# Dense build of a graph kernel: one-hot tiles stored with two pairs innermost instead of one pair's columns side by side

## The chip, the cores and the metric

The kernel runs on one core of a Trainium2 chip. The metric is the device time of one execution in microseconds. Three executions of the kernel before took 9198.9, 9200.97 and 9202.02 us, so the median is 9200.97 us.

## The reference, cut to what matters

The reference is a stack of four graph networks on 3125 nodes with 128 features (three attention layers, an edge network, two further attention layers and two convolutions), all over the same 100,000 edges:

```python
edge_index = jnp.stack([src, dst])
h = jnp.maximum(_layernorm(x, axis=-1), 0.0)
x = x + _L0_gnn_ref(h, edge_index, ...)   # per layer: softmax over the edges of a node, weighted sum of h[src]
...
# L3: per layer, msg = h[row] * dinv[row] * edge_weight * dinv[col]; agg = segment_sum(msg, col)
```

The first and the last network need, of the edges, only how many there are from each source to each destination, and the sum of their weights. The kernel therefore builds two dense matrices once, of 3200 x 3200 entries (25 x 25 cells of 128 x 128): the logarithm of the edge counts (`log_counts`) and the summed weights (`edge_weights`). Later passes read them from memory. The change touches that build alone.

## The kernel before

First the edges are sorted into cells, one cell for each block of 128 destinations and block of 128 sources. The sorted edges of a cell are cut into "pairs": a pair is a column of up to 128 edges together with the cell it belongs to. There is room for 1536 pairs. `spread_pairs` leaves, for each pair, five bf16 numbers per edge in `c.pair[:, 0..4, pair]`: the source within its block, the destination within its block, and the weight cut into three bf16 parts.

`dense_tiles` (line 678 on) then runs five engines side by side, in 96 batches of `PB = 16` pairs:

- **VectorE** writes `hot[k]`, five one-hot tiles per pair of 128 columns each, into one of two buffers, k being the batch number modulo 2. Tiles 0 and 1 compare the column numbers `iotan` with the source and the destination (L740 for the first two batches, L729 in the loop). Tiles 2 to 4 multiply tile 1 by a weight part (L744, and L733 in the loop). So there are five TENSOR_TENSOR instructions of 2048 elements per partition in a batch, 480 in all. One operand is always `value`, the numbers of `c.pair`, broadcast over the 128 columns with the column dimension innermost. Before a batch in the loop (`heat`, L724) the engine waits until TensorE has used up the batch two before, which lay in the same buffer.
- **TensorE** takes each pair of a finished batch with four bf16 matmuls of 128 x 128 x 128: three (L772) add the weights and one (L774) adds the counts. They accumulate in one of five PSUM tiles of the ring `ps`. That makes 64 matmuls per batch. Each reads one pair's tile of `hot` as the stationary operand and another as the moving one. Every fourth pair waits until ScalarE has cleared the PSUM tile.
- **ScalarE** copies each finished cell out of PSUM (L803), clears the tile of the cell before (L789), and takes the logarithm of five cells at once (L793). There are 625 cells, in 125 runs of five.
- **GpSimd** marks empty entries of each run of five cells (L714) and adds the mark to the logarithm (L717).
- **SyncE** stores each run with two DMAs of 320 KB (L819, L822).

Before the loop, GpSimd makes the constants, the first of them being `iotan` (L700, an iota of 128 numbers), and everyone waits for them. The heart of the loop before:

```python
value = c.pair[:, m, at].unsqueeze(2).to_broadcast([P, PB, P])
ve.tensor_tensor(hot[k][:, m, :, :], iotan[:, :].unsqueeze(1).to_broadcast([P, PB, P]), value, ALU.is_equal)
ins = ve.tensor_tensor(hot[k][:, m, :, :], hot[k][:, 1, :, :], value, ALU.mult)
...
pe.matmul(tile[:, 0:P], hot[k][:, 0, j, :], hot[k][:, m, j, :], start=False, stop=m == 4, skip_group_check=True)
pe.matmul(tile[:, P:2 * P], hot[k][:, 1, j, :], hot[k][:, 0, j, :], start=False, stop=True, skip_group_check=True)
```

Of the kernel before, what the change touches and what calls it, by code (L numbers as in the profile page):

```python
# [16 lines left out]
BF16 = mybir.dt.bfloat16  # L17
# [7 lines left out]
P = 128  # L25
# [27 lines left out]
PB = 16  # L53
# [623 lines left out]
def dense_tiles(nc, c, counts, weights):  # L677
# [4 lines left out]
    with ExitStack() as ctx:  # L682
        sb, pb = buffers(nc, ctx)
        iotan = sb("iotan", [P, P], BF16)
        hot = [sb(f"hot{k}", [P, 5, PB, P], BF16) for k in range(2)]
# [7 lines left out]
        with phase(nc, "consts", "hots", "hot_ready", "opened", "paired", "cleared", "copied", "marked", "begun",  # L693
# [3 lines left out]
            with nc.Block() as block:  # L697
                @block.gpsimd
                def _(g):
                    g.iota(iotan[:, :], [[1, P]], base=0, channel_multiplier=0,  # L700
# [19 lines left out]
                def _(ve):  # L720
                    ve.wait_ge(consts, 5)

                    def heat(n, k):
                        ve.wait_ge(paired, (n - 1) * PB)  # L724
                        at = bass.ds(n * PB, PB)
                        for m in range(5):
                            value = c.pair[:, m, at].unsqueeze(2).to_broadcast([P, PB, P])
                            if m < 2:
                                ve.tensor_tensor(hot[k][:, m, :, :], iotan[:, :].unsqueeze(1).to_broadcast([P, PB, P]), value, ALU.is_equal).then_inc(hots, 1)  # L729
                            else:  # L730
                                if m == 2:
                                    ve.wait_ge(hots, 2 * n + 2)
                                ins = ve.tensor_tensor(hot[k][:, m, :, :], hot[k][:, 1, :, :], value, ALU.mult)  # L733
                        ins.then_inc(hot_ready, 1)
                    for n in range(2):
                        at = slice(n * PB, (n + 1) * PB)
                        for m in range(5):
                            value = c.pair[:, m, at].unsqueeze(2).to_broadcast([P, PB, P])
                            if m < 2:
                                ve.tensor_tensor(hot[n][:, m, :, :], iotan[:, :].unsqueeze(1).to_broadcast([P, PB, P]), value, ALU.is_equal).then_inc(hots, 1)  # L740
                            else:
                                if m == 2:
                                    ve.wait_ge(hots, 2 * n + 2)
                                ins = ve.tensor_tensor(hot[n][:, m, :, :], hot[n][:, 1, :, :], value, ALU.mult)  # L744
# [6 lines left out]
                def _(pe):  # L751
# [4 lines left out]
                    with pe.Fori(0, BATCHES // 2) as i:  # L756
                        for k in range(2):
# [9 lines left out]
                            for j in range(PB):  # L767
# [3 lines left out]
                                for m in range(2, 5):  # L771
                                    pe.matmul(tile[:, 0:P], hot[k][:, 0, j, :], hot[k][:, m, j, :], start=False, stop=m == 4,  # L772
                                              skip_group_check=True)
                                pe.matmul(tile[:, P:2 * P], hot[k][:, 1, j, :], hot[k][:, 0, j, :], start=False, stop=True,  # L774
# [1257 lines left out]
```

## Time and profile before

| | |
|---|---|
| median of three runs | 9200.97 us |
| the profiled execution, own time | 9195.21 us |
| its span, first to last instruction | 9193.5 us |
| mean granted TensorE clock, whole span | 0.883 |
| busy: TensorE / VectorE / ScalarE / GpSimd | 6159.8 / 6077.5 / 3756.6 / 4016.8 us |
| dense build, first VectorE instruction to last store issued | 1402.9 to 2716.7 us |

Times in the profile are microseconds from the start of the span unless marked ns. A row of grouped instructions gives the line, the engine, the operation, `out<-in`, shapes (partitions x elements), the count, busy time and mean length in ns, and after the second bar the idle time of the engine just before them with what ended it. PEld is the weight load of TensorE, PE its matmul. The lengths of PE instructions overlap in the pipeline, so their rate is read from start to start.

### The profile page before, as it was taken

The numbers are of one execution on the slowest core, as the hardware profiler recorded it, in microseconds if no ns is written. First come the engines' busy times: TensorE is split into PE (matmuls) and PEld (weight loads), VectorE is DVE, ScalarE is ACT, GpSimd is POOL, SyncE is SP. The second block draws the span as 40 slices with busy tenths as digits, with TensorE's granted clock in tenths as the row PEclk, the third lists the DMA queues.
The fourth block names the chain that finished last, engine by engine and source line by source line (L and its number), as shares of the span: only waits on it lengthen the run. The fifth ranks groups of instructions, "written<-read, shape, count | busy, mean of one in ns | idle before, by whom it ended". The sixth has DMA issues, their size and how long they took to land. (4 is left out here: it accounts for less than half of the span.)

```text
span 9193.5 us, 178963 instructions
## 1 busy us (share of the span) xinstructions
PE 6159.8 (67%) x53418; PEld 5203.8 (57%) x53419; DVE 6077.5 (66%) x16562; ACT 3756.6 (41%) x8315; POOL 4016.8 (44%) x3723
## 2 busy tenths in 40 slices
PE   2222254444447676769999858888885888888766
PEld 2222224433437676747777637777774777777566
DVE  7444429999976565644444458888886888888722
ACT  1111101344536565634544435455543554555410
POOL 3777702456640000037777435555552555555300
PEclk9999997666668888879999979999997999999888
DMA  4111130112213232323333411111113111111345
GB/s 160 52 52 52 52 134 23 57 67 77 80 60 129 87 128 83 113 50 75 73 73 72 45 30 38 37 38 37 37 37 25 41 37 37 38 38 37 27 181 187
DMA packets 472947, 619.50 MB, mean 67 GB/s; under 512 B 283562, under 2 KB 381655, under 8 KB 453589
## 3 DMA queue, kind: packets, MB, share of 16 engines
q1 hardware_dynamic: 362948, 414.53, 13.6%
q0 software_dynamic: 109568, 200.53, 10.3%
q14 instruction: 320, 2.61, 0.1%
q8 instruction: 111, 1.82, 0.1%
HBM read 468.42 MB, written 146.37 MB: 67 GB/s over the span
## 5 line engine op out<-in xcount | busy, mean ns | idle before, releaser
L976 POOL DMA_INDIRECT rows<-source_table,idxb x2640 | 2540.4, 962 | 3043.5 <-ACT idxb L996 1314.6
L1589 DVE CUSTOM_DVE_ANT_0 junk<-pen,ps_top 128x512 f32<-128x512 f32 x1760 | 1136.3, 682 | 140.1 <-PE ps_top L1745 139.6
L772 PE MATMUL ps_cells<-hot 128*128 128x128 bf16 x4608 | 576.1, 284 | 716.3 <-DVE hot L733 629.0
L772 PEld LDWEIGHTS ps_cells<-hot 128*128 128x128 bf16 x4608 | 464.5, 133 | 755.9 <-issue 751.8
L360 POOL DMA_INDIRECT records<-recb,idxb x784 | 762.8, 973 | 256.0 <-issue 246.5
L733 DVE TENSOR_TENSOR hot<-hot,pair 128x2048 bf16<-128x2048 bf16 x282 | 778.1, 2812 | 13.4
L714 POOL TENSOR_SCALAR none<-logs 128x640 f32<-128x640 f32 x125 | 459.2, 3673 | 616.2 <-ACT logs L793 612.9
L1745 PE MATMUL ps_top<-srow,sel 128*128 128x128 bf16 x7040 | 622.6, 224 | 124.5 <-ACT srow L1649 93.1
L388 PE MATMUL ps_g<-hott 64*128 64x128 bf16 x784 | 101.1, 308 | 718.9 <-ACT hott L404 714.8
L1745 PEld LDWEIGHTS ps_top<-srow,sel 128*128 128x128 bf16 x7040 | 448.6, 104 | 233.1 <-issue 153.2
L1708 PEld LDWEIGHTS ps_e<-ident,rows 128*128 128x128 f32 x3520 | 522.5, 213 | 77.0 <-issue 18.9
L1081 PE MATMUL ps_acc<-rows,pt 128*128 128x131 f32 x3750 | 560.0, 296 | 0.0
L803 ACT ACTIVATE both<-ps_cells 128x256 f32<-128x256 f32 x625 | 236.0, 381 | 722.1 <-PE ps_cells L774 715.6
L1759 PE MATMUL ps_acc<-val,hot 128*128 128x132 f32 x3520 | 505.2, 288 | 32.9 <-DVE val L1551 32.4
L1002 PE MATMUL ps_tgt<-identb,dlob 128*128 128x128 bf16 x2640 | 340.4, 231 | 275.3 <-issue 172.1
L1708 PE MATMUL ps_e<-ident,rows 128*128 128x128 f32 x3520 | 519.3, 297 | 3.9 <-DMA rows<-source_table,idxb 3.9
L1093 PE MATMUL ps_t<-ident,y 128*128 128x128 f32 x1875 | 345.9, 311 | 261.0 <-ACT y L1122 261.0
L1081 PEld LDWEIGHTS ps_acc<-rows,pt 128*128 128x128 f32 x3750 | 518.6, 211 | 0.0
L1644 ACT ACTIVATE dist<-ps_tgt,minus_p 128x512 f32<-128x512 f32 x440 | 302.3, 687 | 509.5 <-PE ps_tgt L1002 508.6
L1548 DVE TENSOR_TENSOR val<-rows,p 128x512 f32<-128x512 f32 x440 | 304.8, 693 | 311.0 <-issue 309.3
L388 PEld LDWEIGHTS ps_g<-hott 64*128 64x128 bf16 x784 | 75.2, 138 | 742.1 <-ACT hott L404 739.1
L729 DVE TENSOR_TENSOR hot<-iotan,pair 128x2048 bf16<-128x2048 bf16 x188 | 494.6, 2669 | 0.0
(311 smaller groups left out, 15449.7 us busy)
## 6 DMA issues: line engine op xcount, KB each, us to landing
logs<-log_counts SPq DMA_DIRECT2D x75, 1600.0 KB
wt<-edge_weights SPq DMA_DIRECT2D x50, 1600.0 KB
rows<-source_table,idxb POOLq DMA_INDIRECT x2640
edge_weights<-both SPq DMA_DIRECT2D x125, 320.0 KB, 2.8
log_counts<-none SPq DMA_DIRECT2D x125, 320.0 KB, 2.2
records<-blank SPq DMA_DIRECT2D x16, 1870.0 KB
feat<-records SPq DMA_DIRECT2D x220, 128.0 KB, 2.4
rb<-records SPq DMA_DIRECT2D x6, 4352.0 KB
```

What stands on the lines that cost most here:

```text
L360: g.indirect_dma_start(out=recs[:, :], out_offset=bass.IndirectOffsetOnAxis(ap=idxb[k][:, t:t + 1], axis=0), in_=recb[k][:, t, :], in_offs ...
L714: g.tensor_scalar(none[r][:, :, :], logs[r][:, :, :], -1.0, -BIG, ALU.is_lt, ALU.mult).then_inc(marked, 1)
L729: ve.tensor_tensor(hot[k][:, m, :, :], iotan[:, :].unsqueeze(1).to_broadcast([P, PB, P]), value, ALU.is_equal).then_inc(hots, 1)
L733: ins = ve.tensor_tensor(hot[k][:, m, :, :], hot[k][:, 1, :, :], value, ALU.mult)
L772: pe.matmul(tile[:, 0:P], hot[k][:, 0, j, :], hot[k][:, m, j, :], start=False, stop=m == 4, skip_group_check=True)
L976: g.indirect_dma_start(out=rows[r][:, k, :], out_offset=None, in_=table, in_offset=bass.IndirectOffsetOnAxis(ap=idxb[r][:, k:k + 1], axis= ...
L1081: ins = pe.matmul(ps_acc[b % 2][:, 0:GA], pt[n % 4][:, t, :], c.rows[:, at, 0:GA], start=at == 0, stop=at == NB - 1)
L1093: ins = pe.transpose(ps_t[n % 4][:, t, :], y[b % 2][:, at * P:(at + 1) * P], c.ident[:, :])
L1589: ve.tensor_tensor_reduce(out=junk[h % 2][:, :], in0=pen[mk][:, :], in1=ps_top[h % 2][:, :], scale=1.0, scalar=-BIG, op0=ALU.add, op1=ALU.max,
L1708: ins = pe.matmul(ps_e[:, q * P:(q + 1) * P], rows[r][:, q, :], c.ident[:, :], start=False, stop=q == TG - 1)
L1745: ins = pe.matmul(ps_top[h % 2][:, q * P:(q + 1) * P], sel[:, q * HEADS + h, :], srow[:, :], start=True, stop=True)
L1759: ins = pe.matmul(ps_acc[:, 0:HEADS * HW], hot[r][:, q, :], val[k][:, q * HEADS:(q + 1) * HEADS, :].rearrange("p h f -> p (h f)"), start=q ...
```

## The change

The tiles of a batch are stored as 8 couples of pairs, and within a couple the two pairs' values alternate element by element: column 0 of both pairs, column 1 of both, and so on. `iotan` doubles to 128 x 2 elements, each column number twice. The broadcast `value` now has the couple's two numbers innermost, repeated over 128 columns. TensorE reads one pair out of a couple with a step of two elements (4 bytes). Counts, shapes in elements, waits and order of all instructions stay as they were.

```diff
-        iotan = sb("iotan", [P, P], BF16)
-        hot = [sb(f"hot{k}", [P, 5, PB, P], BF16) for k in range(2)]
+        iotan = sb("iotan", [P, P, 2], BF16)
+        hot = [sb(f"hot{k}", [P, 5, PB // 2, P, 2], BF16) for k in range(2)]
...
-                    g.iota(iotan[:, :], [[1, P]], base=0, channel_multiplier=0,
+                    g.iota(iotan[:, :, :], [[1, P], [0, 2]], base=0, channel_multiplier=0,
...
-                            value = c.pair[:, m, at].unsqueeze(2).to_broadcast([P, PB, P])
+                            value = c.pair[:, m, at].rearrange("p (a j) -> p a j", j=2).unsqueeze(2).to_broadcast([P, PB // 2, P, 2])
                             if m < 2:
-                                ve.tensor_tensor(hot[k][:, m, :, :], iotan[:, :].unsqueeze(1).to_broadcast([P, PB, P]), value, ALU.is_equal).then_inc(hots, 1)
+                                ve.tensor_tensor(hot[k][:, m, :, :, :], iotan[:, :, :].unsqueeze(1).to_broadcast([P, PB // 2, P, 2]), value, ALU.is_equal).then_inc(hots, 1)
                             else:
                                 if m == 2:
                                     ve.wait_ge(hots, 2 * n + 2)
-                                ins = ve.tensor_tensor(hot[k][:, m, :, :], hot[k][:, 1, :, :], value, ALU.mult)
+                                ins = ve.tensor_tensor(hot[k][:, m, :, :, :], hot[k][:, 1, :, :, :], value, ALU.mult)
...
-                                    pe.matmul(tile[:, 0:P], hot[k][:, 0, j, :], hot[k][:, m, j, :], start=False, stop=m == 4,
+                                    pe.matmul(tile[:, 0:P], hot[k][:, 0, j // 2, :, j % 2], hot[k][:, m, j // 2, :, j % 2], start=False, stop=m == 4,
                                               skip_group_check=True)
-                                pe.matmul(tile[:, P:2 * P], hot[k][:, 1, j, :], hot[k][:, 0, j, :], start=False, stop=True,
+                                pe.matmul(tile[:, P:2 * P], hot[k][:, 1, j // 2, :, j % 2], hot[k][:, 0, j // 2, :, j % 2], start=False, stop=True,
                                           skip_group_check=True).then_inc(paired, 1)
```

The first two batches (L740, L744) change in the same way.

## Rows read from the trace of the kernel before

**Rows 1.** The page: the span, and busy time of each engine
```profile
span 9193.5 us, 178963 instructions
PE 6159.8 (67%) x53418; PEld 5203.8 (57%) x53419; DVE 6077.5 (66%) x16562; ACT 3756.6 (41%) x8315; POOL 4016.8 (44%) x3723
```
**Rows 2.** The loop: PE, PEld, DVE, ACT, POOL busy, TensorE clock, DMA share, GB/s
```profile
1425.00:2704.00 1279.00, 577.01 (x6016) 538.49 (x6016) 1265.57 (x471) 542.45 (x1417) 670.38 (x248) 0.67 0.18 64
```
**Rows 3.** Groups of instructions by line, 1400 to 2720 us
```profile
L733 DVE TENSOR_TENSOR hot<-hot,pair 128x2048 bf16<-128x2048 bf16 x282 | 778.1, 2812 | 13.4
L772 PE MATMUL ps_cells<-hot 128*128 128x128 bf16 x4608 | 576.1, 284 | 716.3 <-DVE hot L733 629.0 <-ACT ps_cells L789 72.4 <-DVE hot L744 14.5
L729 DVE TENSOR_TENSOR hot<-iotan,pair 128x2048 bf16<-128x2048 bf16 x188 | 494.6, 2669 | 0.0
L717 POOL TENSOR_TENSOR none<-none,logs 128x640 f32<-128x640 f32 x125 | 215.1, 1721 | 22.9 <-POOL none L714 22.6 <-ACT logs L793 0.4
```
**Rows 4.** VectorE in order of time, two late batches with GpSimd idle
```profile
2681.49 4.49 DVE L729 TENSOR_TENSOR hot<-iotan,pair 128x2048 bf16<-128x2048 bf16 x2
2692.73 4.49 DVE L729 TENSOR_TENSOR hot<-iotan,pair 128x2048 bf16<-128x2048 bf16 x2
```
**Rows 5.** VectorE in order of time, two instructions beside GpSimd
```profile
2318.14 2.80 DVE L733 TENSOR_TENSOR hot<-hot,pair 128x2048 bf16<-128x2048 bf16 x1
2320.87 3.62 DVE L733 TENSOR_TENSOR hot<-hot,pair 128x2048 bf16<-128x2048 bf16 x1
```
**Rows 6.** The line L729: shortest/median/longest ns, first and last start
```profile
L729 DVE TENSOR_TENSOR hot<-iotan,pair x188: 2275/2280/3626, 1425.2 to 2694.9; 128x2048 bf16<-128x2048 bf16 x188
```
**Rows 7.** Groups by line and shape on VectorE, 0 to 130 us
```profile
L238 DVE TENSOR_TENSOR hot<-iota,vals 128x1024 bf16<-128x1024 bf16 x49 | 56.2, 1219 | 0.2
L258 DVE SCALAR_TENSOR_TENSOR meta<-blk_f,meta 128x784 f32<-128x784 f32 x1 | 1.6, 1558 | 0.0
```
**Rows 8.** Groups by line and shape on VectorE, 1150 to 1400 us
```profile
L586 DVE TENSOR_SCALAR past<-at,first 25x1536 bf16<-25x1536 f32 x25 | 25.1, 1007 | 36.1 <-PE ps_b L604 36.1
```
**Rows 9.** The line L714: shortest/median/longest ns, first and last start
```profile
L714 POOL TENSOR_SCALAR none<-logs x125: 2347/3974/4490, 1445.3 to 2712.3; 128x640 f32<-128x640 f32 x125
```
**Rows 10.** TensorE in order of time, one batch; every pair ends in L774
```profile
2681.86 0.50 PE L772 MATMUL ps_cells<-hot 128*128 128x128 bf16 x3 [5.47 <-DVE hot L733]
2682.15 0.32 PE L774 MATMUL ps_cells<-hot 128*128 128x128 bf16 x1
2682.58 0.32 PE L774 MATMUL ps_cells<-hot 128*128 128x128 bf16 x1
2686.69 0.22 PE L774 MATMUL ps_cells<-hot 128*128 128x128 bf16 x1
2686.92 0.22 PE L774 MATMUL ps_cells<-hot 128*128 128x128 bf16 x1
```
**Rows 11.** TensorE in order of time, f32 matmuls at 1375 us
```profile
1374.56 11.33 PE L672 MATMUL ps_x<-pick,mt 128*128 128x512 f32 x26
```
**Rows 12.** Busy time by stretch, 1200 to 1400 us, columns of rows 2
```profile
1200.00:1400.00 200.00, 124.83 (x291) 48.27 (x291) 57.46 (x103) 2.20 (x10) 12.84 (x13) 0.97 0.23 83
```
**Rows 13.** Groups of instructions by line, 2319 to 2419 us
```profile
L714 POOL TENSOR_SCALAR none<-logs 128x640 f32<-128x640 f32 x14 | 49.8, 3560 | 38.1 <-ACT logs L793 37.7
L772 PE MATMUL ps_cells<-hot 128*128 128x128 bf16 x348 | 46.1, 292 | 52.7 <-DVE hot L733 36.9 <-ACT ps_cells L789 15.8
L729 DVE TENSOR_TENSOR hot<-iotan,pair 128x2048 bf16<-128x2048 bf16 x14 | 41.5, 3002 | 0.0
```
**Rows 14.** Groups of instructions by line, 1425 to 1525 us
```profile
L729 DVE TENSOR_TENSOR hot<-iotan,pair 128x2048 bf16<-128x2048 bf16 x18 | 41.7, 2356 | 0.0
L714 POOL TENSOR_SCALAR none<-logs 128x640 f32<-128x640 f32 x3 | 9.4, 3138 | 89.2 <-ACT logs L793 89.2
```
**Rows 15.** Busy time by stretch, a late one, columns of rows 2
```profile
2350.00:2450.00 100.00, 45.12 (x449) 41.01 (x448) 99.00 (x36) 55.16 (x146) 61.06 (x25) 0.62 0.23 79
```

More of the change, by code:

```diff
@@ L737, in _ @@
                         for m in range(5):
-                            value = c.pair[:, m, at].unsqueeze(2).to_broadcast([P, PB, P])
+                            value = c.pair[:, m, at].rearrange("p (a j) -> p a j", j=2).unsqueeze(2).to_broadcast([P, PB // 2, P, 2])
                             if m < 2:
-                                ve.tensor_tensor(hot[n][:, m, :, :], iotan[:, :].unsqueeze(1).to_broadcast([P, PB, P]), value, ALU.is_equal).then_inc(hots, 1)
+                                ve.tensor_tensor(hot[n][:, m, :, :, :], iotan[:, :, :].unsqueeze(1).to_broadcast([P, PB // 2, P, 2]), value, ALU.is_equal).then_inc(hots, 1)
                             else:
@@ L743, in _ @@
                                     ve.wait_ge(hots, 2 * n + 2)
-                                ins = ve.tensor_tensor(hot[n][:, m, :, :], hot[n][:, 1, :, :], value, ALU.mult)
+                                ins = ve.tensor_tensor(hot[n][:, m, :, :, :], hot[n][:, 1, :, :, :], value, ALU.mult)
                         ins.then_inc(hot_ready, 1)
```

## The prediction

> **What bounds the kernel now.** I read the page first, for whose time it is. The span of 9193.5 us holds many passes, and no engine is busy for more than 67% of it [rows 1]: what counts is the dense build alone. The view by stretch comes next. From 1425 to 2704 us VectorE is busy 1265.6 of 1279 us, TensorE 577 and ScalarE 542 [rows 2]. Third, the groups of that stretch show who waits: VectorE's two groups have almost no idle time, while TensorE idled 629 us for `hot` from L733 and 72 us for cleared PSUM tiles [rows 3]. So VectorE sets the pace: 94 batches in 1279 us, 13.6 us each. In order of time, a batch takes 2692.73 - 2681.49 = 11.24 us when GpSimd is quiet [rows 4]. The rest of the 13.6 us is stretching: next to GpSimd's work one instruction took 2.80 and the next 3.62 us [rows 5] where 2.28 is usual [rows 6], so a run of five cells (one L714, one L717) adds 0.52 + 1.34 = 1.86 us to VectorE. 125 runs [rows 3] give 233 us, and 94 x 11.24 + 233 = 1290 us, about the stretch.
>
> **The change, part by part.**
>
> *VectorE, 480 instructions.* From 1024 to 2048 elements TENSOR_TENSOR goes from 1219 [rows 7] to 2280 ns [rows 6]: 1.036 ns per element, with a fixed part of about 158 ns. That is one element per step. A faster pace exists for other instructions here: L586 takes 1007 ns for 1536 elements [rows 8], 0.55 ns each after the same fixed part. No TENSOR_TENSOR in this trace shows it, so the price lies between 2280 ns (no gain; an effect below that is another rival) and half the streaming, 2280 - 1061 = 1219 ns. What distinguishes the old operands is `value`: its innermost dimension repeats one element; after the change all operands have two adjacent elements innermost. I take 1219 ns, because the change removes just the operand that did not advance, and L586 is the nearest row with all operands advancing. It saves 1.061 us x 5 = 5.3 us per batch; a quiet batch falls to 5.94 us, and 480 x 1.061 = 509 us is the most the path can give while the stretching stays.
>
> The Trainium skill, "Vector Engine (DVE) Microarchitecture Reference", section 5.1, says that two-source instructions on 2-byte data pass two elements per cycle when every operand's innermost step is 1 with more than one element, and stay at one where an operand repeats one element. The old rows agree with the second half (2280 ns); no run here shows the first.
>
> *Stretching by GpSimd.* L714 takes 2.35 us at the shortest, 3.97 at the median and 4.49 at the longest [rows 9]: the difference of up to 2.1 us is about the time until the running VectorE instruction ends. What it then takes from VectorE is GpSimd's own reading, which the change leaves alone. I keep 1.86 us per run (233 us). Bounds: none of it, or all of it.
>
> *TensorE's reads, step of 4 bytes.* A pair takes 2682.58 - 2682.15 = 0.43 us at the lower of the clock's two levels (1.2 GHz) and 2686.92 - 2686.69 = 0.23 us at the upper (2.4 GHz) [rows 10]. That is 16 x 0.43 = 6.9 us for a cold batch, plus 0.37 us from VectorE's end to the first matmul (2681.86 after 2681.49) [rows 4, 10]. No bf16 matmul here reads with a step. The nearest row is f32, also a 4-byte step: 26 matmuls of 512 columns in 11.33 us at a granted clock of 0.97, 0.85 ns per column [rows 11, 12], against 0.23 / 4 / 128 = 0.45 ns. So the bounds are no cost and twice the time. 
>
> *Who is next.* Late, 100 us hold 7 batches (14 L729) and about 13.5 runs [rows 13], so 1.9 runs a batch. VectorE would need 5.94 + 1.9 x 1.86 = 9.5 us. TensorE: 45.12 / 7 = 6.4 us busy [rows 15], 15.8 / 7 = 2.3 us waits for cleared tiles [rows 13], 0.37 us start: 9.1 us. GpSimd: 2.35 us for L714 [rows 9], 1.72 for L717 and 0.18 of waiting between them [rows 3], so 4.25 us per run, up to 1.1 more for the shorter VectorE instruction in flight: 8.1 to 10.2 us. ScalarE: 55.16 us busy in 100, 7.9 us a batch [rows 15]. Three engines within a microsecond or so, tied through two `hot` buffers and five PSUM tiles, cannot overlap perfectly. Early, 9 batches have 3 runs [rows 14]: VectorE 5.94 + 0.6 = 6.6 us, TensorE cold 6.9 + 0.4 = 7.2 us, so TensorE sets the pace there.
>
> *Small edits.* `iotan` doubles to 256 numbers on GpSimd, at most 0.3 us ahead of the loop, uncovered. Stores, waits and queues are as before; SyncE stores the same 250 blocks faster, and a DMA share of 0.23 late [rows 15] is far from full even when doubled.
>
> *Sum.* VectorE alone: 94 x 5.94 + 233 = 791 us. About 25 early batches at 0.6 us more for TensorE: 15 us. For near ties in the other 70, 6% of some 9 us each (my estimate, nothing in the trace gives it): 40 us. Together 846 us against 1279: 433 saved. The first two batches save 10 x 1.06 = 10.6 us, the iota gives back 0.3. 9195.2 (the profiled execution's own time; span 9193.5) - 443 = 8752; the median of the runs is 6 us above, so **8758 us**.
>
> **Rivals.**
>
> *The overlap is better, or stretching shrinks with the shorter instructions.* For it: GpSimd's wait for the running instruction must shrink. Against: its reads stay. Without losses 9201 - 519 = 8682; with a quarter less stretching 8624.
>
> *TensorE reads at half rate.* For it: the f32 row. Pairs take 0.46 to 0.86 us. At the upper clock that is 7.4 us a batch and nothing changes; at the present 0.67 of the clock, 0.69 x 16 = 11 us and with start and part of the clear waits 12, saving 94 x 1.6 + 10 = 160: 9040. But TensorE would be busy nearly throughout, and a stretch in which it was 62% busy had 0.97 granted [rows 12]. With 0.85, 0.54 x 16 + 0.4 + 1.2 = 10.2 us: 9201 - 94 x 3.4 - 10 = 8870.
>
> *Nothing happens:* VectorE stays at one element per step, 2280 ns. For it: no TENSOR_TENSOR here ever went faster. 9201.
>
> *Fast, but the steps hop.* L258 reads and writes with gaps of 16 bytes and takes 1558 ns for 784 elements, 1.79 ns each [rows 7]. Should re-reading one couple of numbers cost as much per step, 1024 steps x 1.79 + 158 = 1.99 us: 480 x 0.29 = 139 us saved, 9062. The same Trainium skill page, section 5.2, speaks so against the change: full rate only in runs of two adjacent 4-byte words, 1.73 ns per step with one source hopping every time; by it the time would be about this. The old `value` re-reads one element at full rate, which the trace puts against it.
>
> *Slower.* The mechanism is that hop on VectorE without the fast pace: half a hop per element, 2048 x (1.036 + 0.38) + 158 = 3.06 us, 480 x 0.78 = 374 us: 9575. It decides as soon as an instruction exceeds 2.28 us. Against it: the destination and the first operand stay contiguous, and the old `value`, which did not advance either, had no such penalty [rows 6].
>
> **How the numbers follow.** Forecast 0.53, better overlap 0.14, TensorE at half rate 0.16, hopping but fast 0.05, nothing 0.06, slower 0.06. Faster: 0.88; same (within 0.2%, 18 us, about what a measurement can tell) 0.06; slower 0.06. The range goes from 8630, a quarter less stretching, to 8900, just past half rate at 0.85: it leaves out the last three cases and the tails, under 2 in 10.
>
> **What would show it.** L729 and L733 quiet at about 1.22 us, longest 2.6; VectorE 80 to 95% busy in a loop of about 850 us; TensorE's wait for L733 far below 629 us and its wait for L789 above 72; pairs still 0.43 and 0.23 us apart; L714's longest near 3.4 us; the rest of the span unchanged. Wrong if L729 stays at 2.28 us, if pairs take 0.46 us or more at the upper clock, or if TensorE's waits for cleared tiles swallow the gain.

## The result and the profile after

The kernel after takes 8734.99 us (median of 4 runs, 8730.65 to 8746.85) against 9199.93 us for the kernel before (4 runs, 9195.02 to 9202.02): a ratio of 0.9497, with a 95% interval of 0.9481 to 0.9514. That is 5.0% faster. The forecast was 8758 us, in a range of 8630 to 8900. The profiled execution of after took 8746.85 us, at a mean granted clock of 0.904.

The page of the kernel after, its span and the engines' busy time, answers to [rows 1]:

```profile
span 8745.1 us, 178963 instructions
PE 6104.3 (70%) x53418; PEld 5137.0 (59%) x53419; DVE 5536.3 (63%) x16562; ACT 3756.5 (43%) x8315; POOL 3951.0 (45%) x3723
```

VectorE lost 541 us of busy time and TensorE 55; the counts of instructions are the same. The loop of the dense build now runs from 1419.8 to 2249.2 us, 829 us instead of 1279 [rows 2]. The groups of that stretch (1400 to 2260 us) answer to [rows 3]:

```profile
L772 PE MATMUL ps_cells<-hot 128*128 128x128 bf16 x4608 | 517.4, 258 | 315.2 <-ACT ps_cells L789 181.4 <-DVE hot L733 67.3 <-issue 61.5
L733 DVE TENSOR_TENSOR hot<-hot,pair 128x2048 bf16<-128x2048 bf16 x282 | 441.7, 1619 | 13.4
L714 POOL TENSOR_SCALAR none<-logs 128x640 f32<-128x640 f32 x125 | 365.5, 2924 | 235.0 <-ACT logs L793 230.4
L729 DVE TENSOR_TENSOR hot<-iotan,pair 128x2048 bf16<-128x2048 bf16 x188 | 295.5, 1612 | 83.5 <-PE ps_cells L774 83.4
L803 ACT ACTIVATE both<-ps_cells 128x256 f32<-128x256 f32 x625 | 236.4, 382 | 279.0 <-PE ps_cells L774 265.7 <-issue 10.7
L717 POOL TENSOR_TENSOR none<-none,logs 128x640 f32<-128x640 f32 x124 | 230.0, 1854 | 22.7 <-POOL none L714 22.4 <-ACT logs L793 0.4
```

Three things are to be seen. TensorE's wait for `hot` from L733 fell from 629 to 67 us. Its wait for cleared PSUM tiles rose from 72 to 181. And VectorE, which waited for nothing before, now waits 83 us for TensorE to free a buffer. Nobody is the sole bound any more. The same instructions line by line (count, shortest/median/longest ns), answering to [rows 6, 9]:

```profile
L729 DVE TENSOR_TENSOR hot<-iotan,pair x188: 1209/1226/2576, 1419.8 to 2244.3; 128x2048 bf16<-128x2048 bf16 x188
L714 POOL TENSOR_SCALAR none<-logs x125: 2348/3048/3433, 1433.5 to 2258.1; 128x640 f32<-128x640 f32 x125
L772 PE MATMUL ps_cells<-hot x4608: 217/230/312, 1413.4 to 2255.8; 128*128 128x128 bf16 x192
```
Three stretches of 100 us (columns as in [rows 2]) show the loop change its character as the cells get emptier and more runs of cells fall on a batch:

```profile
1425.00:1525.00 100.00, 67.31 (x935) 61.50 (x936) 97.67 (x73) 37.22 (x95) 37.10 (x16) 0.91 0.15 52
1725.00:1825.00 100.00, 60.58 (x704) 54.10 (x704) 87.70 (x55) 70.03 (x184) 76.76 (x33) 0.81 0.31 105
2025.00:2125.00 100.00, 57.32 (x608) 50.56 (x608) 74.30 (x47) 76.93 (x202) 81.62 (x35) 0.72 0.32 109
```

Early, VectorE is still the bound (97.67 of 100 us). Late, no engine is over 82%, and 10 batches (20 L729) pass in 100 us where 7 did [rows 13]. There the groups of 2025 to 2125 us read:

```profile
L772 PE MATMUL ps_cells<-hot 128*128 128x128 bf16 x456 | 55.3, 269 | 41.2 <-ACT ps_cells L789 33.1 <-issue 8.1
L729 DVE TENSOR_TENSOR hot<-iotan,pair 128x2048 bf16<-128x2048 bf16 x20 | 30.7, 1576 | 24.5 <-PE ps_cells L774 24.5
L803 ACT ACTIVATE both<-ps_cells 128x256 f32<-128x256 f32 x89 | 33.6, 382 | 21.6 <-PE ps_cells L774 19.9 <-issue 1.5
```

TensorE waits for ScalarE (33.1), ScalarE waits for TensorE (19.9), and VectorE waits for TensorE (24.5): a ring through the five PSUM tiles, in which each is late for the other by turns.

Where did the 448 us between the two profiled executions come from? The loop gives 449.5. The two batches ahead of it give 9.7, since they take 12.6 instead of 22.3 us. The longer iota takes back 1.3 (1.53 us for 256 numbers where it was 0.24 for 128). Ahead of the build this execution was 3.0 us later, and behind it some 6 us longer, in passes that the change doesn't touch. One of these, the long pass from line 1704 on, is the same within 2 us (5418.0 to 8679.6 us before, 4967.5 to 8230.7 after).

### The profile page after: what moved, and what is told of

The parts are those of the page before. It is cut to its first block and busy times, and to the rows that moved or that the text cites. A ratio compares the mean times of both kernels' runs of the same rounds, so it can differ in the third digit from the quotient of the medians.

```text
span 8745.1 us, 178963 instructions
## 1 busy us (share of the span) xinstructions
PE 6104.3 (70%) x53418; PEld 5137.0 (59%) x53419; DVE 5536.3 (63%) x16562; ACT 3756.5 (43%) x8315; POOL 3951.0 (45%) x3723
## 5 line engine op out<-in xcount | busy, mean ns | idle before, releaser
L772 PE MATMUL ps_cells<-hot 128*128 128x128 bf16 x4608 | 517.4, 258 | 315.2 <-ACT ps_cells L789 181.4
L772 PEld LDWEIGHTS ps_cells<-hot 128*128 128x128 bf16 x4608 | 386.2, 117 | 368.3 <-issue 354.1
L1649 ACT ACTIVATE srow<-ps_srow 128x128 bf16<-128x128 bf16 x440 | 122.2, 278 | 847.3 <-PE ps_srow L1727 847.3
L714 POOL TENSOR_SCALAR none<-logs 128x640 f32<-128x640 f32 x125 | 365.5, 2924 | 235.0 <-ACT logs L793 230.4
L1767 PE MATMUL ps_sc<-att,lr 128*128 128x4 f32 x3520 | 460.6, 254 | 12.9 <-DVE lr L1576 12.9
L1759 PEld LDWEIGHTS ps_acc<-val,hot 128*128 128x128 f32 x3520 | 441.6, 195 | 41.9 <-ACT hot L1659 36.2
```

Of the source, the lines that this page charges most:

```text
L714: g.tensor_scalar(none[r][:, :, :], logs[r][:, :, :], -1.0, -BIG, ALU.is_lt, ALU.mult).then_inc(marked, 1)
L772: pe.matmul(tile[:, 0:P], hot[k][:, 0, j // 2, :, j % 2], hot[k][:, m, j // 2, :, j % 2], start=False, stop=m == 4, skip_group_check=True)
L1759: ins = pe.matmul(ps_acc[:, 0:HEADS * HW], hot[r][:, q, :], val[k][:, q * HEADS:(q + 1) * HEADS, :].rearrange("p h f -> p (h f)"), start=q ...
L1767: ins = pe.matmul(ps_sc[:, q * HEADS:(q + 1) * HEADS], lr[:, q * P:(q + 1) * P], att4[:, :], start=True, stop=True)
```

## The experiments

Nearly all rest on one of two bases, whose own price was measured, because they differ from the changed kernel at two register loads. TensorE loads four numbers `until` per batch and ScalarE five numbers `last` per run of cells into registers (each is the value that a wait compares with). These loads run on the engine's sequencer, the part that hands the engine its instructions. In the first base, every loaded value is asserted to lie within its range; in the second, the wait compares with the larger of the value and zero. "Matmul stretch" below is the time from the first to the last start of the fourth matmul of a pair (L774 in the kernel after): 1295.4 us before, 842.2 after.

### The base with assertions, and the same on the kernel before

```diff
-    c.until[...], engines=[pe.engine], min_val=1, max_val=NB * CELLS,
-    skip_runtime_bounds_check_because="a cell's number and one")
+    c.until[...], engines=[pe.engine], min_val=1, max_val=NB * CELLS)
...
-    c.last[...], engines=[act.engine], min_val=1, max_val=PAIRS,
-    skip_runtime_bounds_check_because="the number of pairs before a cell's end")
+    c.last[...], engines=[act.engine], min_val=1, max_val=PAIRS)
```

> The changed kernel with the two register loads of TensorE (until) and ScalarE (last) asserted to lie in their bounds, which adds a few sequencer instructions per batch; nothing else. It is the base of the experiments that follow. If the assertions are hidden, the time is the changed kernel's 8735 us within 0.3%. If TensorE's sequencer is on the path (its idle time put down to issue was 61 us in the dense build), up to 96 x 0.3 us = 30 us more, up to 8765 us.

> The kernel before with the same two asserted loads. VectorE sets its pace and everything else waits, so all theories expect no difference from the kernel before, 9200 us within 0.2%.

Measured: on the changed kernel 8880.86 us, ratio to before 0.9658 (0.9642 to 0.9675), some 146 us slower than without them, where at most 30 were expected. On the kernel before, 9191.40 us, ratio 0.9999 (0.9990 to 1.0009): nothing, as expected. The instructions of the `until` line and of the `last` line in the changed kernel with assertions, over the whole run and then in one batch and one run of cells:

```profile
L762 PEldq FUSED_REGOPS  x480: 46/146/174, 1407.8 to 2401.8; - x160
L762 PEldq SEQ_ASSERT  x384: 18/18/28, 1408.5 to 2402.0; - x192
L796 ACTq FUSED_REGOPS  x725: 52/147/168, 1409.7 to 2365.5; - x182
L796 ACTq SEQ_ASSERT  x625: 18/18/29, 1409.9 to 2365.7; - x157
```
```profile
L762 PEldq SEQ_ASSERT  x4: 18/18/18, 2055.9 to 2056.7; - x4
L796 ACTq SEQ_ASSERT  x5: 18/18/18, 2055.2 to 2056.1; - x5
```

The two instructions of an assertion are busy for 0.146 + 0.018 = 0.164 us, but from start to start one takes its sequencer more: 0.85 / 3 = 0.28 us on TensorE's (2055.88 to 2056.73) and 0.90 / 4 = 0.22 on ScalarE's (2055.24 to 2056.14). 384 of them are about 108 us on TensorE's, 625 about 140 on ScalarE's. The groups, 1400 to 2410 us:

```profile
L771 PE MATMUL ps_cells<-hot 128*128 128x128 bf16 x4608 | 565.4, 274 | 417.2 <-ACT ps_cells L788 264.2 <-issue 146.5 <-DVE hot L744 3.9
L729 DVE TENSOR_TENSOR hot<-iotan,pair 128x2048 bf16<-128x2048 bf16 x188 | 271.1, 1482 | 267.3 <-PE ps_cells L773 267.1
```

TensorE idles 102 us more (417.2 against 315.2), 85 of it as "issue", which is its own sequencer, and 83 for ScalarE, less the 67 it had spent on `hot`. Its matmuls are busy 48 us longer (565.4 against 517.4), as the mean granted clock of the loop fell from 0.78 to 0.70. 102 + 48 = 150 us, about the 146 that the time shows. On the kernel before, with the same assertions (1400 to 2720 us), TensorE's idle time doesn't grow, 707.5 us where it was 716.3 [rows 3]. Its wait for `hot` is 540 us instead of 629, its wait for cleared tiles 150 instead of 72:

```profile
L771 PE MATMUL ps_cells<-hot 128*128 128x128 bf16 x4608 | 583.8, 285 | 707.5 <-DVE hot L733 540.0 <-ACT ps_cells L788 150.4 <-DVE hot L744 14.2
```

So the pair of runs gives the plainest evidence of where the bound went: a cost on the sequencers of TensorE and ScalarE was hidden behind VectorE before, and costs time after. A third of that time comes through the lower clock and not through the sequencers. The 108 us on TensorE's sequencer would alone be enough for its 102 us of idle time; which of the two sequencers carries it wasn't separated.

### TensorE reading adjacent elements

```diff
+def flat(k, m, j):
+    return hot[k][:, m, j // 2, :, :].rearrange("p f j -> p (f j)")[:, (j % 2) * P:(j % 2 + 1) * P]
...
-pe.matmul(tile[:, 0:P], hot[k][:, 0, j // 2, :, j % 2], hot[k][:, m, j // 2, :, j % 2], ...)
+pe.matmul(tile[:, 0:P], flat(k, 0, j), flat(k, m, j), ...)
```

> after_checked, but TensorE reads 128 adjacent elements of a couple in place of every second one (the products are then of mixed pairs; that part of the result is other than the reference). VectorE's work is as in after_checked. Theory (a 4-byte step costs TensorE nothing): pairs stay 0.43 and 0.23 us apart and the time is after_checked's within 0.2%. Rival (the step costs something and is part of why TensorE is late): warm pairs come closer together than in after_checked, whose stretches show 0.23 to 0.25 us, and the time falls by 5 to 30 us.

The fourth matmul of a pair changes in the same way. Measured: 8884.87 us (ratio 0.9660, 0.9644 to 0.9676), the base's 8880.86 within its spread, as the theory had it. TensorE in time order with adjacent reads, at the upper clock:

```profile
1510.34 0.22 PE L776 MATMUL ps_cells<-hot 128*128 128x128 bf16 x1
1510.56 0.22 PE L776 MATMUL ps_cells<-hot 128*128 128x128 bf16 x1
```

and the kernel after, with the 4-byte step, a pair at the lower clock and one at the upper:

```profile
1503.33 0.31 PE L774 MATMUL ps_cells<-hot 128*128 128x128 bf16 x1
1503.76 0.31 PE L774 MATMUL ps_cells<-hot 128*128 128x128 bf16 x1
1504.13 0.22 PE L774 MATMUL ps_cells<-hot 128*128 128x128 bf16 x1
1504.36 0.22 PE L774 MATMUL ps_cells<-hot 128*128 128x128 bf16 x1
```

0.43 and 0.23 us apart, as in [rows 10]. With adjacent reads the pairs at the lower clock are 0.43 us apart too (1699.97 and 1700.40 us in that run). The step of 4 bytes is free.

### Eight pairs innermost: a 16-byte step for TensorE

```diff
-        iotan = sb("iotan", [P, P, 2], BF16)
-        hot = [sb(f"hot{k}", [P, 5, PB // 2, P, 2], BF16) for k in range(2)]
+        iotan = sb("iotan", [P, P, 8], BF16)
+        hot = [sb(f"hot{k}", [P, 5, PB // 8, P, 8], BF16) for k in range(2)]
...
-pe.matmul(tile[:, 0:P], hot[k][:, 0, j // 2, :, j % 2], hot[k][:, m, j // 2, :, j % 2], ...)
+pe.matmul(tile[:, 0:P], hot[k][:, 0, j // 8, :, j % 8], hot[k][:, m, j // 8, :, j % 8], ...)
```

> after_checked with eight pairs innermost in place of two: VectorE's operands run over eight adjacent elements, TensorE reads with a step of 16 bytes. VectorE: 1220 ns as now in all theories. TensorE, theory (a step costs nothing as long as each read is one element per clock): pairs 0.43 and 0.23 us apart and the time within 0.3% of after_checked. Rival (a step of a whole 16-byte line costs, as the line rule of the Trainium skill, SBUF - State Buffer, Door 1, has it): warm pairs at 0.3 us or more and the dense build 50 to 400 us longer.

`value` and the fourth matmul change in the same way. Measured: 9365.38 us, ratio 1.0188 (1.0171 to 1.0205), 1.9% above the kernel before and 484 us above the base, more than the 400 that the rival allowed. VectorE's L729 is untouched (1209/1225 ns); TensorE in time order, its weight loads and matmuls over the loop, then the window of the loop:

```profile
1700.09 0.41 PE L773 MATMUL ps_cells<-hot 128*128 128x128 bf16 x1
1701.03 0.41 PE L773 MATMUL ps_cells<-hot 128*128 128x128 bf16 x1
```
```profile
L771 PEld LDWEIGHTS ps_cells<-hot x4608: 141/146/173, 1412.5 to 2884.8; 128*128 128x128 bf16 x192
L771 PE MATMUL ps_cells<-hot x4608: 407/414/434, 1412.5 to 2885.0; 128*128 128x128 bf16 x192
```
```profile
1430.00:2860.00 1430.00, 1403.99 (x5963) 863.40 (x5962) 621.37 (x468) 557.14 (x1417) 523.08 (x248) 0.50 0.16 57
```

Pairs are 0.94 us apart, 2.2 times the 0.43 of the lower clock. The Trainium skill, "SBUF — State Buffer", section "Door 1: The DMA port swizzle", has accesses that cross from one 16-byte line to another pay a penalty unless a line is hit twice. Both runs agree: a step of 4 bytes cost nothing, one of 16 bytes 0.51 us per pair at the lower clock. No step between the two was run. Both operands have the step, but only the matmuls are longer, 0.41 us where 0.31 is usual at this clock; the weight loads keep 0.15, which points to the read of the moving operand. The second thing in that window is for later: TensorE is busy 1404 of 1430 us, and the granted clock stays at 0.50, the lower level.

### A column table that isn't doubled

```diff
-        iotan = sb("iotan", [P, P, 2], BF16)
+        iotan = sb("iotan", [P, P], BF16)
...
-ve.tensor_tensor(hot[k][:, m, :, :, :], iotan[:, :, :].unsqueeze(1).to_broadcast([P, PB // 2, P, 2]), value, ...)
+ve.tensor_tensor(hot[k][:, m, :, :, :], iotan[:, :].unsqueeze(1).unsqueeze(3).to_broadcast([P, PB // 2, P, 2]), value, ...)
```

> after_checked, but the column numbers are stored once and repeated for the two pairs of a couple by a step of 0 in the innermost dimension; hot and value keep their layout. Only the two comparisons per batch (L729) have such an operand. Theory (every operand must advance in its innermost dimension for the double pace): L729 goes back to about 2280 ns, L733 stays at 1220, the loop's VectorE work grows by 192 x 1.06 = 204 us, of which 83 us of VectorE's present waits can absorb a part: total 120 to 200 us above after_checked. Rival (only the second operand, or only the written layout, decides): L729 stays at 1220 ns and the time stays.

Measured: 8927.21 us, 0.9711 (0.9694 to 0.9727), 46 us above the base, where 120 to 200 were expected. The two lines of one kernel, side by side:

```profile
L729 DVE TENSOR_TENSOR hot<-iotan,pair x188: 2276/2797/3641, 1421.0 to 2436.3; 128x2048 bf16<-128x2048 bf16 x188
L733 DVE TENSOR_TENSOR hot<-hot,pair x282: 1209/1224/2572, 1425.6 to 2441.0; 128x2048 bf16<-128x2048 bf16 x141
```

One operand out of two that stands still innermost is enough for one element per step. VectorE's L729 became 244 us dearer (515.4 against 271.1), yet the time rose by 46 only: VectorE's wait for TensorE fell from 267 to 70 us and took the rest. The expectation had allowed for 83 us of such waits, the figure of the kernel after, while the base has 267.

### The pair table doubled, the old layout of `hot` kept

```diff
-        iotan = sb("iotan", [P, P, 2], BF16)
-        hot = [sb(f"hot{k}", [P, 5, PB // 2, P, 2], BF16) for k in range(2)]
+        iotan = sb("iotan", [P, P], BF16)
+        hot = [sb(f"hot{k}", [P, 5, PB, P], BF16) for k in range(2)]
...
+        pair2 = sb("pair2", [P, 5, PAIRS, 2], BF16)
...
+                    for j in range(2):
+                        ve.tensor_copy(pair2[:, :, :, j], c.pair[:, :, :]).then_inc(twice, 1)
...
-  value = c.pair[:, m, at].rearrange("p (a j) -> p a j", j=2).unsqueeze(2).to_broadcast([P, PB // 2, P, 2])
+  value = pair2[:, m, at, :].unsqueeze(2).to_broadcast([P, PB, P // 2, 2])
```

> The old layout of hot and iotan, contiguous columns per pair and contiguous reads on TensorE, but each number of the pair table is stored twice (two copies at the start of the dense build, 2 x 7680 elements), so that value has two adjacent equal elements innermost. Theory (the double pace needs only that every operand advances over two elements; the layout of hot does not matter): L729 and L733 at about 1220 ns, the loop as in after_checked, plus 8 to 17 us for the copies, of which up to 14 us are hidden while VectorE waits for the constants: 0 to 20 us above after_checked. Rival (the layout of the tiles itself matters): 2280 ns and 9200 us.

The matmuls and the other `hot` operands go back to the kernel before, two adjacent columns being taken as the innermost dimension of each. Measured: 8877.97 us, 0.9661 (0.9645 to 0.9678), equal to its base, as the theory had it. The line that was L729:

```profile
L733 DVE TENSOR_TENSOR hot<-iotan,pair x188: 1209/1225/2558, 1424.3 to 2395.5; 128x2048 bf16<-128x2048 bf16 x188
```

The fast pace doesn't come from the layout of `hot`. It comes from `value` having two adjacent elements innermost instead of one repeated; the same number twice does as well as two pairs' numbers. The loop starts 5.5 us later for the copying.

### GpSimd that only writes

```diff
-g.tensor_scalar(none[r][:, :, :], logs[r][:, :, :], -1.0, -BIG, ALU.is_lt, ALU.mult).then_inc(marked, 1)
+g.memset(none[r][:, :, :], 0.0).then_inc(marked, 1)
...
-g.tensor_tensor(none[r][:, :, :], none[r][:, :, :], logs[r][:, :, :], ALU.add).then_inc(masked[r], 1)
+g.memset(none[r][:, :, :], 1.0).then_inc(masked[r], 1)
```

> after_checked, but GpSimd's two instructions per run of five cells only write constants (two memsets of 640 elements) and read nothing; the logarithms of the counts are left out of the stored matrix. Theory (what stretches VectorE is GpSimd reading): no VectorE instruction of the loop is above 1.3 us, VectorE's busy time in the loop falls from about 737 us by some 175 us to 560, and the dense build by 30 to 120 us, as TensorE and ScalarE then hold it. Rival (writes stretch it as well): VectorE instructions of 1.7 us and more remain, in number about as many as before.

Measured: 8898.25 us, 0.9686 (0.9670 to 0.9702), 17 us slower than its base, where 30 to 120 less were expected. VectorE's instructions, and the group with its wait:

```profile
L729 DVE TENSOR_TENSOR hot<-iotan,pair x188: 1217/1222/1227, 1410.1 to 2411.5; 128x2048 bf16<-128x2048 bf16 x188
```
```profile
L729 DVE TENSOR_TENSOR hot<-iotan,pair 128x2048 bf16<-128x2048 bf16 x188 | 221.9, 1222 | 443.1 <-PE ps_cells L773 443.1
```

Not one instruction is stretched: the longest is 1227 ns, where its base had 2558. So GpSimd's writes of the same tiles do nothing to VectorE, and the stretching goes with what was taken away, most plainly the reads. The memsets are also shorter (0.63 us each) and do no arithmetic, and that wasn't separated from the reads. The removal took 151 us of busy time from VectorE while the time didn't fall: the wait for TensorE grew by 176. On this base the stretching is off the path. The matmul stretch even grew by 26 us, from 993.8 to 1020.2, and began 9 us earlier, which makes the 17; TensorE's "issue" time rose from 146.5 to 166.9 us there. Why is open.

### Three buffers instead of two

```diff
-        hot = [... for k in range(2)]
+        hot = [... for k in range(3)]
...
-                        ve.wait_ge(paired, (n - 1) * PB)
+                        ve.wait_ge(paired, (n - 2) * PB)
...
-                    with ve.Fori(1, BATCHES // 2) as i:
-                        for k in range(2):
-                            heat(2 * i + k, k)
+                    with ve.Fori(1, BATCHES // 3) as i:
+                        for k in range(3):
+                            heat(3 * i + k, k)
```

> after_checked with three hot buffers in place of two, VectorE waiting for the batch three before. Theory (in the late part VectorE and TensorE hold each other up through two buffers: VectorE waited 83 us for TensorE and TensorE 67 us for VectorE): most of the smaller of the two goes, 30 to 70 us less than after_checked. Rival (ScalarE, through the five PSUM tiles, sets the late pace: TensorE waited 181 us for cleared tiles): VectorE only runs further ahead and waits later, the time falls by less than 15 us.

TensorE's loop is unrolled by three as well. Measured: 8786.22 us, 0.9558 (0.9542 to 0.9574), 95 us under its base. It looks like a success for the buffers, and isn't. The matmul stretch is only 12 us shorter (981.4 against 993.8), as the rival had it. In time order, TensorE found its next batch full at all 95 changes of batch instead of 78, and still stood 3.0 us on average. The rest is in a pass that has no `hot` of this kind. The weight loads of its line 1702, first in the kernel with two buffers, then in that with three:

```profile
L1702 PEld LDWEIGHTS ps_e<-hott,mine x1320: 95/96/152, 5113.2 to 8366.3; 128*128 x189
```
```profile
L1702 PEld LDWEIGHTS ps_e<-hott,mine x1320: 95/96/152, 5101.7 to 8275.7; 128*128 x189
```

3253 against 3174 us, 79 of the 95. In the nine other kernels that ran on chips of this speed, with 319 to 321 of the packets below, this pass takes 3241 to 3266 us, so 79 us is no scatter. Among the queues' rows on the pages one differs much, the packets of instructions that the program fetched, 320 against 195:

```profile
q14 instruction: 320, 2.62, 0.1%
```
```profile
q14 instruction: 195, 1.60, 0.1%
```

That unrolling by three moved the later code and spared fetches is my reading; only the counts are shown.

### The second base, and register loads moved earlier

These ran on another chip, on which the kernel before takes 10702.15 us. The passes with indirect DMAs are longer there (the long pass takes 4184 us in the kernel with maxima, 3263 in the kernel after), the dense build hardly. Savings in microseconds compare roughly with those above, ratios don't.

```diff
-                                    pe.wait_ge(cleared, until[j // 4])
+                                    pe.wait_ge(cleared, smax(until[j // 4], 0))
...
-                            act.wait_ge(paired, last[q])
+                            act.wait_ge(paired, smax(last[q], 0))
```

> The changed kernel, with the two kinds of registers bounded by a maximum with zero at each wait (one register operation each) in place of the assertions of after_checked (two checks for every value right behind the load). Theory (what made after_checked 146 us slower than the changed kernel is TensorE's sequencer: its loads of turn, 1.1 us, and until, 0.33 us, and what follows them lie between two batches and are on the path): the maxima lie at the waits, where the sequencer mostly has queued work ahead of it, so the dense build is 60 to 150 us shorter than in after_checked, 8735 to 8820 us in all. Rival (ScalarE's assertions cost it, 125 loads of 5 values): the same gain here, so this run alone doesn't tell; but then the two runs with earlier loads on TensorE gain nothing against this one.

(The bounds declared at the loads also go from 1 to -1.) Measured: 10254.15 us, 448 saved, 0.9589 (0.9569 to 0.9609); the changed kernel saved 465 and the first base 309. The matmul stretch is 849.3 us against the 842.2 of the kernel after, 144 less than in the first base, as the theory had it (60 to 150). This base is nearly the changed kernel itself, so the price of the first one was the assertions. On it, two kernels let TensorE load the next batch's numbers in the middle of a batch, one with two batches unrolled in the loop, the other with four:

```diff
+                                if j == 8 and q < 2 - 1:
+                                    held = loads(n + 1)
...
-                        for k in range(2):
-                            n = 2 * i + k
-                            _, turn = nc.values_load_multi_w_load_instructions(...)
-                            _, until = nc.values_load_multi_w_load_instructions(...)
+                        held = loads(2 * i)
+                        for q in range(2):
+                            n, k = 2 * i + q, q % 2
+                            turn, until = held
```

> bounded_by_max, with TensorE's loads of turn and until for the second batch of each loop iteration issued in the middle of the first one, ahead of its wait for a cleared tile at the ninth pair; the first batch's stay at the top. Theory (the loads between batches are on the path): in 48 of 96 batches 1.4 to 1.8 us of sequencer time moves under queued matmuls or a wait for ScalarE; 20 to 60 us less than bounded_by_max. Rival (the loads are hidden, ScalarE sets the pace): within 5 us.

> As early_loads_2 with four batches per iteration of TensorE's loop, so that 72 of 96 batches have their loads early. Theory: one and a half times the gain of early_loads_2, 30 to 90 us less than bounded_by_max. Against it: the loop's code is twice as long, and instruction fetches at its end may give part back.

Measured: 10273.72 us (0.9608, 0.9588 to 0.9629) and 10255.04 us (0.9589, 0.9569 to 0.9608), with matmul stretches of 862.9 and 852.4 us. Neither gains, where 20 to 60 and 30 to 90 us were expected. The edit did move the pauses: in time order, TensorE's pauses between batches are 215 us in all in the base, 163 with two batches unrolled and 122 with four. But the batches themselves grew longer by as much or more. In the groups TensorE waits 315.8 and 314.4 us in all, against 305.8 in the base: the "issue" part of the first fell from 64.9 to 40.6 and the wait for `hot` rose from 49.8 to 81.0, while in the second "issue" rose to 74.1. A load has to run on the sequencer at some time, and in the middle of a batch it stands ahead of matmuls too; that this is all of it is my reading. By the expectation of the second base, no gain here speaks for ScalarE's assertions as what the first base paid for; since the moved loads cost time inside the batches, it doesn't settle that.

### One load for a row of cells, with three buffers

```diff
+                        _, last = nc.values_load_multi_w_load_instructions(
+                            c.last[0:1, bass.ds(b * CELLS, CELLS)], engines=[act.engine], ...)
                         for u in range(CELLS):
...
-                                _, last = nc.values_load_multi_w_load_instructions(
-                                    c.last[0:1, bass.ds(b * CELLS + u, RUN)], engines=[act.engine], ...)
...
-                            act.wait_ge(paired, smax(last[q], 0))
+                            act.wait_ge(paired, smax(last[u], 0))
```

> bounded_by_max with two edits: ScalarE loads the 25 values of last for a row of cells in one instruction in place of five loads of 5 (1.12 us each at the median, 125 of them), and three hot buffers. Three buffers were worth 13 us of the dense build in three_hot. Theory (every microsecond of ScalarE's sequencer stands in the ring TensorE - ScalarE - TensorE, as the assertions did that cost 150 us): some 90 us of loads go, and VectorE's loop, 836 us from L729's first start to L733's last end in bounded_by_max, takes 740 to 790 us. Rival (the loads lie behind the logarithm of the run before and are hidden; only what is added to TensorE's sequencer counts): 810 to 830 us. The whole kernel is faster than the changed one in either case if the later passes stay as they are; in three_hot they were 80 us shorter beside, at the same number of instructions but 125 fewer instruction fetches.

Measured, on another chip again: 10238.36 us, and the kernel before took 10693.76 beside it, 0.9587 (0.9572 to 0.9602), 455 saved. The matmul stretch grew to 886.6 us, 37 more than in its base, so the build got worse, against both the theory and the rival, and other passes better. TensorE's wait for cleared tiles rose from 186.0 to 219.7 us and its "issue" time from 64.9 to 124.0. The load, in this kernel and in the kernel after:

```profile
L795 ACTq TENSOR_LOAD <-last x25: 1713/6642/7570, 1634.9 to 2465.1; - x25
```
```profile
L797 ACTq TENSOR_LOAD <-last x125: 534/1122/2539, 1409.9 to 2218.3; - x125
```

25 numbers at once take 6.64 us, no less than five loads of 1.12, and they come in one piece, which I read as more than the five PSUM tiles can bridge; the two edits were not run apart. The fetches fell again, to 194, but the 79 us didn't come with them: here the long pass was 16 us shorter. No kernel that I ran is clearly better than the changed one.

## Why the prediction was right, and where it was off

**The instruction.** Predicted 1219 ns, measured 1226 at the median, so the step that took L586's pace for a TENSOR_TENSOR stood. The reason given for it, operands that advance, was then shown twice: L729 falls back to 2276 ns when the column table alone stands still, and keeps 1225 ns in the old layout with doubled numbers. The Trainium skill, "Vector Engine (DVE) Microarchitecture Reference", section 5.1, asks of two-source instructions on 2-byte data an innermost step of one over more than one element in every operand, and the measurements agree in both directions. The rate rule in section 5.2 of the same page of the Trainium skill (4-byte words in adjacent twos, or 1.73 ns per step with one source hopping) would have given the hop rival; re-reading one couple of bf16 numbers showed no such price here.

**The step of TensorE.** Predicted as no cost; shown by adjacent reads taking the same time. A strided read can cost, as the half-rate rival (0.16) had it, but not at this step: it cost 2.2 times the pair at 16 bytes. Its clock was wrong as well. It let the clock rise to 0.85 under a busy TensorE, and the run with eight pairs innermost kept 0.50 at 98% busy.

**The stretching.** Predicted 233 us, kept in full. Measured: VectorE's two groups are busy 737 us. A batch with GpSimd quiet, in time order in the kernel after:

```profile
2230.07 2.36 DVE L729 TENSOR_TENSOR hot<-iotan,pair 128x2048 bf16<-128x2048 bf16 x2 [0.53 <-PE ps_cells L774]
2232.57 3.50 DVE L733 TENSOR_TENSOR hot<-hot,pair 128x2048 bf16<-128x2048 bf16 x3
2235.98 2.35 DVE L729 TENSOR_TENSOR hot<-iotan,pair 128x2048 bf16<-128x2048 bf16 x2
```

The quiet length of 94 batches is 94 x (2.36 + 3.50) = 551 us; the rest is 186. The longest L729 is 2576 ns and L714 fell to 3433 at the longest, as forecast (2.6 and 3.4 us). So the forecast had 47 us too much. Some 11 of them were too much already for the kernel before, where its own sum gave 1290 us for a stretch of 1279 and the same count gives 1273 - 94 x (4.49 + 6.69) = 222 us (the three L733 from 2686.12 us on take 6.69). The other 36 vanished. My reading is that part of GpSimd's work now falls into VectorE's own waits, where it stretches nothing; the kernels with longer such waits agree (267 us of waits and 150 of stretching in the first base, 805 and 74 with eight pairs innermost).

**Who is next.** The sum had 15 us for an early TensorE and 40 for near ties late, 55 in all, and VectorE's wait for TensorE came to 83. The place of it was half right. Early, TensorE never set the pace: VectorE waited 0.3 us for it from 1425 to 1525 us, and the granted clock there was 0.91, not the lower level (1.2 GHz) on which the 7.2 us per batch rested. Late, the near tie was real and larger: 24.5 us of wait per 100.

**The sum.** For the loop, 846 us were forecast and 829 measured. Two errors, 47 too much stretching and 28 too little waiting, mostly cancel: 846 - 47 + 28 = 827. Two more cancel outside the loop: the time outside it was some 11 us worse than forecast (3 ahead of the build, 6 behind it, 1 for the iota, which took 1.3 us longer where 0.3 at most was forecast, and 1 less gained in the first two batches), and the median lay 12 us under the profiled execution where 6 above it was assumed. The prediction is right in its mechanism, and its closeness of 0.3% (23 us) is in part luck. Of the rivals, the one with the best overlap had an error of its own: its 519 us count the 10 of the first two batches twice, since 480 x 1.061 = 509 holds them, so that it should read 8692 and not 8682. Nothing was decided by that.

**What was left out.** The prediction counted busy time and waits, and named nothing of the sequencers. Yet TensorE's loads of `turn` and `until` take 1.11 + 0.33 us at the median in each of the 96 batches:

```profile
L759 PEldq TENSOR_LOAD <-turn x96: 1102/1107/2483, 1407.4 to 2248.6; - x96
L762 PEldq TENSOR_LOAD <-until x96: 328/333/868, 1408.9 to 2249.9; - x96
```

They appear in the groups only as 61.5 us of "issue". In time order, the start of one late batch of the kernel after shows them in their place, with the two loads of that batch below:

```profile
2047.11 2.56 DVE L733 TENSOR_TENSOR hot<-hot,pair 128x2048 bf16<-128x2048 bf16 x1
2050.03 0.22 PE L774 MATMUL ps_cells<-hot 128*128 128x128 bf16 x1
2050.40 2.36 DVE L729 TENSOR_TENSOR hot<-iotan,pair 128x2048 bf16<-128x2048 bf16 x2 [0.73 <-PE ps_cells L774]
2053.01 0.34 PE L772 MATMUL ps_cells<-hot 128*128 128x128 bf16 x3 [2.76 <-issue]
```
```profile
L759 PEldq TENSOR_LOAD <-turn x1: 1981/1981/1981, 2050.1 to 2050.1; - x1
L762 PEldq TENSOR_LOAD <-until x1: 337/337/337, 2052.3 to 2052.3; - x1
```

The last matmul of a batch frees the buffer, VectorE starts at once, and TensorE stands for 2.76 us with its next batch already full (L733 had ended it at 2049.67): `turn` takes 1.98 us here, `until` 0.34. Over the loop, the next batch was full at 42 of the 95 changes of batch, and TensorE stood 2.1 us on average at these, 88 us in all; before the change it was full at none, and such a pause lay inside the wait for `hot`. The experiments with assertions show that time on these sequencers now counts. What exactly sets the late pace stays open: neither earlier loads, nor a third buffer, nor a GpSimd that reads nothing shortened the stretch by more than 13 us, so it isn't any one of these alone. ScalarE has about 9 cells per batch to copy and to clear there (89 L803 in 10 batches) and is busy 77 of 100 us. All these kernels leave that work as it is, so ScalarE's share in the late pace is not tested.

## What to carry to other kernels

When a two-source VectorE instruction on bf16 broadcasts a number, see to it that two elements, different or equal, lie adjacent innermost in every operand: storing the small table twice is enough and leaves the large tile as it is (1225 ns instead of 2280). If the layout of the tile is interleaved instead, keep TensorE's step small: 4 bytes were free here, 16 cost more than the change had gained. And once the bound is gone, price what was under its cover, the register loads and assertions of the sequencers among it: an edit that was free in the slow kernel cost 1.7% in the fast one, and an edit's gain is to be looked up in its own stretch before it is credited.

## What was unexpected of the hardware

- A TensorE that is busy 1404 of 1430 us with matmuls that read at a 16-byte step kept a granted clock of 0.50 throughout, while the same matmuls with free reads, busy 67 of 100 us, had 0.91 (1425 to 1525 us).
- GpSimd's memsets didn't lengthen VectorE's instructions at all (1217 to 1227 ns); the two instructions that read and compute on the same tiles did, by up to 1.35 us.
- A register load costs ScalarE about 0.22 us per number with 5 (1.12 us at the median, 0.53 at the shortest) and 0.27 with 25 (6.64 us), and TensorE 0.07 with 16 (1.11 us).
- An assertion on a loaded register is busy for 0.16 us and takes its sequencer 0.28 us on TensorE and 0.22 on ScalarE, from start to start.
- A third buffer in one pass went with 125 fewer instruction fetches, and a pass 2700 us later that was 79 us shorter.
